# Last graph layer: the probabilities become the stationary operand of the weighing

## The chip, the cores and the metric

The kernel runs on one core of a Trainium2 chip. The metric is the device time of one execution in microseconds (us). Before the change it is 2272.47 us, the median of three runs (2269.34 to 2274.48).

## What is computed

The reference runs four graph layers over 1250 nodes with 512 features and 20,000 edges. The change touches only the last one, a graph attention with 8 heads of 64 features:

```python
for h in range(8):
    Wx = x @ Ws[h] + Wb[h]
    s = leaky_relu(Wx[v_tgt] @ a_w[h, :d] + Wx[v_src] @ a_w[h, d:] + a_b[h], 0.2)
    alpha = _segment_softmax(s, v_tgt, n)
    outs.append(segment_sum(alpha[:, None] * Wx[v_src], v_tgt, num_segments=n))
return stack(outs, axis=1).reshape(n, -1)
...
x = _layernorm(x + _L3_gnn_ref(...))
```

The kernel does this densely: for each head it makes a 1250 x 1250 matrix of exponentials, with the logarithm of the number of edges between two nodes added to the score, and multiplies it with the values Wx. A column of ones beside the values gives the sum of the exponentials, by which the result is divided.

## The kernel before, in words

The layer is `fourth_layer`. Nodes are cut into 10 tiles of 125 (TILE, TILES; HALF is 5). After a set-up (turning the nodes, the score rows, the values `values[source, tile, head, 65]` with their column of ones) come 80 steps: step T is head h = T // 10 and source tile j = T % 10. In a step the 125 sources of the tile lie on the partitions and all 1250 targets along them. All operands of the weighing are fp32, and each fp32 matmul appears in the trace as two passes, that is two weight loads and two matmuls.

One step passes these engines:

- POOL adds the logs of the counts and the targets' shifts (L2033, `logs_and_shifts`, two buffers).
- DVE combines that with the spread target scores in PSUM banks 3 to 5 (L2134, into `probabilities_turned`, four buffers). It waits for POOL, and for the weighing of four steps earlier (`pv`).
- ACT takes the exponential in place (L2208).
- PE weighs (L2307, `weigh`): the values of the tile (125 x 65) are stationary and the 1250 probabilities stream through in cuts of 512, 512 and 226, summed over the ten steps of the head in PSUM banks 0 to 2, 65 partitions by 1250 columns.

DVE has a second task between those: for the head after, it looks for each source tile's peak over the neighbours (L2071, `peaks`, 30 a head: 20 with 512 columns and 10 with 226), reading scores that PE spreads into bank 6 (L2258, `spread_sources`, three times a head). The peaks of a head run six steps ahead. In step j = 4 DVE works out the shifts (`shift_of`, L2079 to L2087), PE turns them (L2276, `shift_turned`) and spreads them in three pieces (L2282, `shift_piece`, steps 5, 6 and 7), all through bank 7, and ACT copies each piece (L2190). At j = 0 PE spreads the target scores of the new head (L2265, `spread_targets`) once DVE's last step of the old head is done.

The end of a head, before the change: ACT copies the 65 x 1250 sums out (L2198, `copy_out`, in step j = 0 of the next head), and the first weighing of the next head waits for that copy, since it writes the same banks. In steps 2 and 3 PE turns the copy back (L2297, `turn_back`, five transposes of 65 x 125 each time) into bank 7, in steps 3 and 4 DVE divides (`out_part`: L2099, L2101, L2106), and in steps 5 and 6 POOL adds the result to the nodes (L2025, `join`). `shift_turned` of the next head shares bank 7 with this and so waits for `parted` of both halves.

The order of the work on every engine is written out by hand. PE's order in a step is: target scores (j = 0), source scores (j = 4, 7, 0), shifts (j = 4) or a piece (j = 5, 6, 7), the weighing of the step before, a turning back (j = 2, 3). After the last step come the copy, the turning back, the division, the join, the row statistics, the norm and the output.

Of the kernel before, what the change touches and what calls it, by code (L numbers as in the profile page):

```python
# [9 lines left out]
ACT = mybir.ActivationFunctionType  # L10
AX = mybir.AxisListType
F32 = mybir.dt.float32
# [5 lines left out]
NODES, DIM, EDGES = 1250, 512, 20000  # L18
TILE = 125
TILES = NODES // TILE  # L20
# [10 lines left out]
CUTS = [(0, 512), (512, 1024), (1024, NODES)]  # L31
# [4 lines left out]
HEADS3, HDIM3 = 8, 64  # L36
# [6 lines left out]
def packer(nc, start):  # L43

    at = [start]

    def place(name, shape, dtype):
        size = int(np.prod(shape[1:])) * (2 if dtype in (BF16, F16) else 4)
        t = nc.alloc_sbuf_tensor_at(name, shape, dtype, offset=SBUF_BASE + at[0])
        at[0] += -(-size // 32) * 32  # L50
        return t

    return place
# [576 lines left out]
LAST_AT = WORK_AT + TILES * DIM * 4 + 640  # L630
# [1291 lines left out]
def fourth_layer(nc, fx, lw, psum, out):  # L1922
# [5 lines left out]
    with ExitStack() as ctx:  # L1928
        def sem(name):
            return ctx.enter_context(nc.semaphore("L3_" + name))  # L1930
# [26 lines left out]
        prob = packer(nc, TURNED_AT)("probabilities_turned", [128, 4, NODES], F32)  # L1957
        shifts = packer(nc, TURNED_AT + PLANE)("target_shifts_spread", [128, 2, NODES], F32)
        offset = packer(nc, SLOT_A_AT + TILES * NODES * 4 + 16)("logs_and_shifts", [128, 2, NODES], F32)
        weighted = packer(nc, LAST_AT)("weighted_values_turned", [128, 2, NODES], F32)  # L1960

        stored = sem("stored")
        turned, x_copied, picked, ones_set = sem("nodes_turned"), sem("turned_copied"), sem("selector_ready"), sem("ones_set")
# [6 lines left out]
        shift_own, shift_ready = sem("shift_step"), sem("shifts_ready")  # L1970
        piece, piece_copied = sem("spread_pieces"), sem("spread_pieces_copied")
        offset_ready, scored, exped, pv = sem("offsets_ready"), sem("scored"), sem("exped"), sem("weighted")
        out_copied, last_copied, back = sem("weighted_copied"), sem("last_weighted_copied"), sem("weighted_turned_back")
        part_own, parted, joined = sem("part_or_row_scale_step"), sem("parts_ready"), sem("nodes_joined")
        stat_own, var_ready, std_ready = sem("stats_step"), sem("variance_ready"), sem("std_ready")
        scale_ready = sem("row_scales_ready")
# [3 lines left out]
        def bank(n):  # L1980
            return psum[:, n * BANK:(n + 1) * BANK]

        def cols(t):
            return slice(t * TILE, (t + 1) * TILE)
# [4 lines left out]
        def region(n):  # L1989
            return psum[:, n * BANK:n * BANK + NODES]  # L1990

        def back_bank(h, k):

            return bank(6 if (h, k) == (HEADS3 - 1, 1) else 7)

        def reach_of(h):

# [3 lines left out]
        PEAKS = 3 * TILES  # L2001
# [39 lines left out]
        def _(dve):  # L2041
# [51 lines left out]

            def out_part(h, k):

                view = back_bank(h, k)[0:TILE, 0:HALF * WIDTH].rearrange("p (t d) -> p t d", d=WIDTH)
                m, v, n = mass[0:TILE, k, :], inverse[0:TILE, k, :], 2 * h + k
                dve.wait_ge(back, n + 1)
                dve.tensor_scalar(m, view[:, :, HDIM3:WIDTH].rearrange("p t d -> p (t d)"), 1e-30, None, ALU.max).then_inc(part_own, 1)  # L2099
                dve.wait_ge(part_own, 2 * n + 1)  # L2100
                dve.reciprocal(v, m).then_inc(part_own, 1)  # L2101
                dve.wait_ge(part_own, 2 * n + 2)
                if h >= 1:

                    dve.wait_ge(joined, n - 1)
                dve.tensor_tensor(part[0:TILE, k], view[:, :, 0:HDIM3], v.unsqueeze(2).broadcast_to([TILE, HALF, HDIM3]),  # L2106
                                  ALU.mult).then_inc(parted, 1)
# [19 lines left out]
            for T in range(STEPS):  # L2127
                h, j = T // TILES, T % TILES
                dve.wait_ge(offset_ready, T + 1)
                if j == 0:  # L2130
                    dve.wait_ge(target_spread, h + 1)
                if T >= 4:
                    dve.wait_ge(pv, T - 3)
                dve.scalar_tensor_tensor(prob[0:TILE, T % 4, :], region(3)[0:TILE], bend[0:TILE, j, h:h + 1],  # L2134
                                         offset[0:TILE, T % 2, :], ALU.max, ALU.add).then_inc(scored, 1)
                if j == TILES - 6 and h < HEADS3 - 1:
                    shift_of(h + 1)
                if h >= 1 and j in (3, 4):
                    out_part(h - 1, j - 3)
                g, at = (T + AHEAD) // TILES + 1, (T + AHEAD) % TILES  # L2140
                if g < HEADS3:
                    for n in range(PEAKS_AT[at], PEAKS_AT[at + 1]):
                        peaks(g, n)
                if h == HEADS3 - 1 and j in STATS_AT:
                    kept_stats(*STATS_AT[j])
            kept_stats(HALF, TILES)
            dve.wait_ge(pv, STEPS)
            a, z = CUTS[1]
            dve.tensor_copy(weighted[0:WIDTH, (HEADS3 - 1) % 2, a:z], region(0)[0:WIDTH, a:z]).then_inc(last_copied, 1)
            for k in range(2):  # L2150
                out_part(HEADS3 - 1, k)

# [21 lines left out]
        def _(act):  # L2174
# [14 lines left out]
                act.wait_ge(piece, 4 * h + 2 + k)  # L2189
                nc.scalar.activation(shifts[0:TILE, h % 2, a:z], bank(7)[0:TILE, 0:z - a], ACT.Copy).then_inc(piece_copied, 1)  # L2190

            def copy_out(h):

                act.wait_ge(pv, TILES * (h + 1))
                if h >= 2:
                    act.wait_ge(back, 2 * h - 2)
                for a, z in ((0, NODES),) if h < HEADS3 - 1 else CUTS[0::2]:
                    nc.scalar.activation(weighted[0:WIDTH, h % 2, a:z], region(0)[0:WIDTH, a:z], ACT.Copy).then_inc(out_copied, 1)  # L2198

            shift_turned(0)  # L2200
            for k in range(3):
                shift_piece(0, k)
# [2 lines left out]
            for T in range(STEPS):  # L2205
                h, j = T // TILES, T % TILES
                act.wait_ge(scored, T + 1)
                nc.scalar.activation(prob[0:TILE, T % 4, :], prob[0:TILE, T % 4, :], ACT.Exp,  # L2208
                                     bias=column[0:TILE, j, HEADS3 + h:HEADS3 + h + 1], scale=1.0 / UNIT3).then_inc(exped, 1)
                if j == 0 and h >= 1:  # L2210
                    copy_out(h - 1)
                if h < HEADS3 - 1:
                    if j == 4:
                        shift_turned(h + 1)
                    if j in (5, 6, 7):
                        shift_piece(h + 1, j - 5)
            copy_out(HEADS3 - 1)
            for k in range(2):
                at = half(k)
                act.wait_ge(var_ready, HALF * (k + 1))  # L2220
# [9 lines left out]
        def _(pe):  # L2230
# [37 lines left out]
            def shift_turned(h):  # L2268
                if h == 0:
                    pe.wait_ge(cols_ready, 2)  # L2270
                elif h == 1:
                    pe.wait_ge(piece_copied, 4)
                else:
                    pe.wait_ge(parted, 2 * h - 2)
                pe.wait_ge(shift_ready, h + 1)
                pe.transpose(bank(7)[0:TILES, 0:TILE], shift[0:TILE, h % 2, :], fx.ident[0:TILE, 0:TILE]).then_inc(piece, 1)  # L2276

# [5 lines left out]
                                   start=True, stop=True)  # L2283
                mm.then_inc(piece, 1)

            def turn_back(h, k):

                pe.wait_ge(out_copied, h + 1 if (h, k) != (HEADS3 - 1, 1) else HEADS3 + 1)
                if h == HEADS3 - 1:
                    pe.wait_ge(last_copied, 1)  # L2290
                    pe.wait_ge(peaked, PEAKS * HEADS3)
                if k == 0:
                    pe.wait_ge(piece_copied, 4 * min(h + 2, HEADS3))
                elif h < HEADS3 - 1:
                    pe.wait_ge(parted, 2 * h + 1)
                for t in range(HALF):
                    mm = pe.transpose(back_bank(h, k)[0:TILE, t * WIDTH:(t + 1) * WIDTH], weighted[0:WIDTH, h % 2, cols(k * HALF + t)],  # L2297
                                      fx.ident[0:WIDTH, 0:WIDTH])
                mm.then_inc(back, 1)

            def weigh(T):
                h, j = T // TILES, T % TILES
                pe.wait_ge(exped, T + 1)
                if j == 0 and h >= 1:
                    pe.wait_ge(out_copied, h)
                for a, z in CUTS:
                    mm = pe.matmul(region(0)[0:WIDTH, a:z], values[0:TILE, j, h, :], prob[0:TILE, T % 4, a:z],  # L2307
                                   start=(j == 0), stop=(j == TILES - 1))
                mm.then_inc(pv, 1)

            value(0)
# [19 lines left out]
            for T in range(STEPS):  # L2331
                h, j = T // TILES, T % TILES
                if j == 0 and h >= 1:
                    spread_targets(h)
                g, at = (T + AHEAD) // TILES + 1, (T + AHEAD) % TILES
                if g < HEADS3 and at in (0, 3, 6):
                    spread_sources(g, at // 3)
                if h < HEADS3 - 1:
                    if j == 4:
                        shift_turned(h + 1)  # L2340
                    if j in (5, 6, 7):
                        shift_piece(h + 1, j - 5)
                if T >= 1:
                    weigh(T - 1)
                if h >= 1 and j in (2, 3):
                    turn_back(h - 1, j - 2)
            weigh(STEPS - 1)
            for k in range(2):
                turn_back(HEADS3 - 1, k)


_INS = ("x", "src", "dst", "edge_weight", "node_vec1", "L0_gnn_W", "L1_gnn_f_w1", "L1_gnn_f_b1", "L1_gnn_f_w2",
# [47 lines left out]
```

## Time and profile before

| | |
|---|---|
| time, median of three runs | 2272.47 us |
| time of the profiled execution | 2274.44 us |
| its span | 2272.7 us |
| last layer's 80 steps, first DVE step to last weighing | 1992.09 to 2254.93 us |
| time from the start of one head's target scores to the next, heads 2 to 5 | 33.98 to 33.99 us each |
| mean granted TensorE clock | 0.968 |

The span is the profiler's, from the first to the last instruction; the time beside it is 1.74 us longer. "Busy" is the time in which an engine had an instruction running. PEclk is the share of the full TensorE clock that was granted: 1.00 is 2.4 GHz, 0.50 is 1.2 GHz. PEld is TensorE's weight load, which can run beside a matmul.

### The profile page before, as it was taken

Reading aid. Unit: us, or ns where it says so; the run is one execution under the profiler, and the core shown is the slowest. Engines: PE = TensorE matmul, PEld = TensorE weight load, DVE = VectorE, ACT = ScalarE, POOL = GpSimd, SP = SyncE. Lnnn points to the kernel's source line nnn. Section 1 sums busy time; section 2 is a strip of 40 time slices with the busy share of each in tenths; the row PEclk is TensorE's granted clock in tenths of the full one; section 3 lists DMA queues with packets and bytes.
Section 4 is the critical chain, followed back from the end, with each engine's and each line's share of the span. In section 5 each row is a group of like instructions: output and inputs, shape, how many; then the busy total and the mean of one; then the engine's idle time right before and its main releaser. Section 6 shows DMA issues by size and latency. Waiting matters only on the chain. (4 is left out here: it accounts for less than half of the span.)

```text
span 2272.7 us, 39837 instructions
## 1 busy us (share of the span) xinstructions
PE 2066.5 (91%) x15006; PEld 1608.6 (71%) x15006; DVE 1573.7 (69%) x3095; ACT 957.0 (42%) x1444; POOL 665.8 (29%) x488
## 2 busy tenths in 40 slices
PE   5999979899899999899999899999898996978886
PEld 4899937788788888788888787888785554433332
DVE  6789754778764778764777765678855235699985
ACT  0222213666333666433666433666420023045444
POOL 0000015300554200554210554200350000088785
PEclk9999989999999999999999999999999997999998
DMA  2000041789711698811688812588963300000001
GB/s 75 24 25 36 32 143 60 133 143 154 157 47 52 120 151 144 171 44 55 112 150 149 177 34 65 99 147 148 205 153 90 68 12 22 0 1 1 0 1 46
DMA packets 490381, 195.82 MB, mean 86 GB/s; under 512 B 441767, under 2 KB 460199, under 8 KB 490195
## 3 DMA queue, kind: packets, MB, share of 16 engines
q1 hardware_dynamic: 490195, 193.31, 41.8%
q8 instruction: 121, 1.98, 0.4%
q14 instruction: 65, 0.53, 0.1%
HBM read 62.94 MB, written 25.45 MB: 39 GB/s over the span
## 5 line engine op out<-in xcount | busy, mean ns | idle before, releaser
L720 PE MATMUL psum<-turned_probability_parts,values_high 125*128 125x125 bf16 x1600 | 278.6, 221 | 49.9 <-DMA turned_probability_parts<-probability_parts 23.2
L922 DVE CUSTOM_DVE_ANT_0 probabilities<-psum,counts 125x1250 f32<-125x1250 f32 x160 | 233.5, 1460 | 114.9 <-PE psum L722 114.6
L1480 ACT ACTIVATE probabilities<-probabilities,row_peaks 125x1250 f32<-125x1250 f32 x160 | 214.5, 1341 | 176.2 <-DVE row_peaks L926 176.2
L722 PE MATMUL psum<-turned_probability_parts,values_low 125*128 125x125 bf16 x1600 | 277.8, 220 | 0.0
L721 PE MATMUL psum<-turned_probability_parts,values_high 125*128 125x125 bf16 x1600 | 277.6, 220 | 0.0
L1680 DVE SCALAR_TENSOR_TENSOR probability_parts<-probabilities,row_masses,probability_parts 125x1250 bf16<-125x1250 f32 x160 | 251.6, 1573 | 13.5 <-ACT probability_parts L1492 13.3
L2033 POOL TENSOR_TENSOR logs_and_shifts<-logs_by_source,target_shifts_spread 125x1250 f32<-125x1250 f32 x80 | 208.2, 2619 | 107.3 <-ACT target_shifts_spread L2190 67.9
L1492 ACT ACTIVATE probability_parts<-probabilities,row_masses 125x1250 bf16<-125x1250 f32 x160 | 214.1, 1338 | 46.4 <-DVE row_masses L934 43.1
L2307 PE MATMUL psum<-probabilities_turned,values_and_ones 125*65 125x512 f32 (+1 forms) x480 | 190.1, 540 | 23.5 <-ACT probabilities_turned L2208 13.1
L720 PEld LDWEIGHTS psum<-turned_probability_parts,values_high 125*128 125x128 bf16 x1600 | 158.0, 99 | 73.8 <-issue 67.9
L2307 PEld LDWEIGHTS psum<-probabilities_turned,values_and_ones 125*65 125x65 f32 x480 | 63.6, 142 | 136.2 <-issue 113.7
L705 ACT ACTIVATE norm_std<-norm_moments,norm_eps 125x1 f32<-125x1 f32 x110 | 32.2, 294 | 299.9 <-DVE norm_moments L701 299.7
L721 PEld LDWEIGHTS psum<-turned_probability_parts,values_high 125*128 125x128 bf16 x1600 | 158.5, 99 | 0.0
L722 PEld LDWEIGHTS psum<-turned_probability_parts,values_low 125*128 125x128 bf16 x1600 | 158.4, 99 | 0.0
L2208 ACT ACTIVATE probabilities_turned<-probabilities_turned,score_columns 125x1250 f32<-125x1250 f32 x80 | 106.8, 1338 | 121.7 <-DVE probabilities_turned L2134 121.6
L457 PE MATMUL psum<-onehot_band,onehot_source 125*128 x2200 | 138.1, 226 | 16.6 <-DVE onehot_band L390 16.6
L457 PEld LDWEIGHTS psum<-onehot_band,onehot_source 125*128 125x128 bf16 x2200 | 131.2, 102 | 17.8 <-issue 17.1
L720 PE MATMUL psum<-turned_high,head_weights 128*128 128x512 f32 (+1 forms) x384 | 137.0, 357 | 3.7 <-POOL head_weights L1080 2.1
L722 PE MATMUL psum<-turned_high,head_weights 128*128 128x512 f32 (+1 forms) x384 | 136.1, 355 | 0.0
L721 PE MATMUL psum<-turned_low,head_weights 128*128 128x512 f32 (+1 forms) x384 | 136.1, 354 | 0.0
L2134 DVE SCALAR_TENSOR_TENSOR probabilities_turned<-psum,source_bends,logs_and_shifts 125x1250 f32<-125x1250 f32 x80 | 121.1, 1515 | 20.8 <-POOL logs_and_shifts L2033 12.9
L2071 DVE CUSTOM_DVE_ANT_0 masked_source_scores<-psum,absent_edges_by_target 125x512 f32<-125x512 f32 (+1 forms) x240 | 128.2, 584 | 9.3 <-PE psum L2258 9.3
(335 smaller groups left out, 5061.0 us busy)
## 6 DMA issues: line engine op xcount, KB each, us to landing
weight_stage<-in_L_gnn_m_w SPq DMA_DIRECT2D x32, 256.0 KB, 2.9
block_inputs_kept<-nodes SPq DMA_DIRECT2D x8, 896.0 KB
counts_kept<-counts_by_target_rows SPq DMA_DIRECT2D x10, 625.0 KB, 3.1
logs_kept<-counts SPq DMA_DIRECT2D x1, 5468.8 KB
nodes<-block_inputs_kept SPq DMA_DIRECT2D x12, 448.0 KB
turned_probability_parts<-probability_parts SPq DMA_TRANSPOSE x320, 3.6
counts_by_target<-counts_kept SPq DMA_DIRECT2D x2, 2187.5 KB
logs_by_source<-logs_kept SPq DMA_DIRECT2D x1, 4375.0 KB
```

What stands on the lines that cost most here:

```text
L457: mm = pe.matmul(region(b)[:, k * 128:(k + 1) * 128], onehot[0:TILE, q, k * TILE:k * TILE + 128], station[0:TILE, bass.ds(at, 1), q, :, :] ...
L720: pe.matmul(out, lh, rh, start=first, stop=False, skip_group_check=True)
L721: pe.matmul(out, lh, rl, start=False, stop=False, skip_group_check=True)
L722: return pe.matmul(out, ll, rh, start=False, stop=last, skip_group_check=True)
L922: dve.tensor_tensor_reduce(prob[0:TILE, T % 2, :], scores, fx.count_src[0:TILE, i, 0:NODES], scale, MASKED, ALU.add, ALU.max, p[:, 0:1]).t ...
L1480: nc.scalar.activation(prob[0:TILE, T % 2, :], prob[0:TILE, T % 2, :], ACT.Exp, bias=fx.peak[0:TILE, T % 2, 1:2], accum_out=fx.mass[0:TILE ...
L1492: nc.scalar.activation(parts[0:TILE, T % 2, 0:TILES, 0:TILE], by_tile(prob[0:TILE, T % 2, :]), ACT.Copy, scale=fx.mass[0:TILE, i, 2:3]).th ...
L1680: dve.scalar_tensor_tensor(parts[0:TILE, T % 2, TILES:2 * TILES, 0:TILE], by_tile(prob[0:TILE, T % 2, :]), fx.mass[0:TILE, i, 2:3], parts[ ...
L2033: nc.gpsimd.tensor_tensor(offset[0:TILE, T % 2, :], lw.logs[0:TILE, j, :], shifts[0:TILE, h % 2, :], ALU.add).then_inc(offset_ready, 1)
L2071: dve.tensor_tensor_reduce(masked[0:TILE, N % 2, 0:z - a], bank(6)[0:TILE, 0:z - a], lw.mask[0:TILE, t, a:z], 1.0, MASKED, ALU.add, ALU.ma ...
L2134: dve.scalar_tensor_tensor(prob[0:TILE, T % 4, :], region(3)[0:TILE], bend[0:TILE, j, h:h + 1], offset[0:TILE, T % 2, :], ALU.max, ALU.add ...
L2307: mm = pe.matmul(region(0)[0:WIDTH, a:z], values[0:TILE, j, h, :], prob[0:TILE, T % 4, a:z], start=(j == 0), stop=(j == TILES - 1))
```

## The change

The two operands of the weighing change places. In `weigh` a 125 x 125 block of the probabilities becomes stationary and the 65 columns of the values stream through it, ten times a step, so that the sums come out with the targets on the partitions: 125 x (5 x 65) for each half of the targets, in one bank. The halves n = 2h + k use banks 0, 1 and 2 in turn. `copy_out`, `turn_back`, the buffer `weighted_values_turned` and their semaphores go. `out_part` reads the sums where PE left them, waits for `pv` of the whole head, and moves from steps 3 and 4 to steps 1 and 2. A weighing that starts a bank for the fourth time or later waits for `parted` of the half that used it before. `shift_turned` no longer waits for `parted`, only for the copies of its own bank.

```diff
-        def back_bank(h, k):
-            return bank(6 if (h, k) == (HEADS3 - 1, 1) else 7)
+        def rows_bank(h, k):
+            return bank((2 * h + k) % 3)
...
             def out_part(h, k):
-                view = back_bank(h, k)[0:TILE, 0:HALF * WIDTH].rearrange("p (t d) -> p t d", d=WIDTH)
+                view = rows_bank(h, k)[0:TILE, 0:HALF * WIDTH].rearrange("p (t d) -> p t d", d=WIDTH)
...
-                dve.wait_ge(back, n + 1)
+                dve.wait_ge(pv, TILES * (h + 1))
...
-                if h >= 1 and j in (3, 4):
-                    out_part(h - 1, j - 3)
+                if h >= 1 and j in (1, 2):
+                    out_part(h - 1, j - 1)
...
-            dve.wait_ge(pv, STEPS)
-            a, z = CUTS[1]
-            dve.tensor_copy(weighted[0:WIDTH, (HEADS3 - 1) % 2, a:z], region(0)[0:WIDTH, a:z]).then_inc(last_copied, 1)
...
-            def copy_out(h):
-                act.wait_ge(pv, TILES * (h + 1))
-                if h >= 2:
-                    act.wait_ge(back, 2 * h - 2)
-                for a, z in ((0, NODES),) if h < HEADS3 - 1 else CUTS[0::2]:
-                    nc.scalar.activation(weighted[0:WIDTH, h % 2, a:z], region(0)[0:WIDTH, a:z], ACT.Copy).then_inc(out_copied, 1)
...
             def shift_turned(h):
                 if h == 0:
                     pe.wait_ge(cols_ready, 2)
-                elif h == 1:
-                    pe.wait_ge(piece_copied, 4)
                 else:
-                    pe.wait_ge(parted, 2 * h - 2)
+                    pe.wait_ge(piece_copied, 4 * h)
...
             def weigh(T):
                 h, j = T // TILES, T % TILES
                 pe.wait_ge(exped, T + 1)
-                if j == 0 and h >= 1:
-                    pe.wait_ge(out_copied, h)
-                for a, z in CUTS:
-                    mm = pe.matmul(region(0)[0:WIDTH, a:z], values[0:TILE, j, h, :], prob[0:TILE, T % 4, a:z],
-                                   start=(j == 0), stop=(j == TILES - 1))
+                for t in range(TILES):
+                    k, at = t // HALF, (t % HALF) * WIDTH
+                    if j == 0 and t % HALF == 0 and 2 * h + k >= 3:
+                        pe.wait_ge(parted, 2 * h + k - 2)
+                    mm = pe.matmul(rows_bank(h, k)[0:TILE, at:at + WIDTH], prob[0:TILE, T % 4, cols(t)], values[0:TILE, j, h, :],
+                                   start=(j == 0 and t % HALF == 0), stop=(j == TILES - 1), skip_group_check=True)
                 mm.then_inc(pv, 1)
...
-                if h >= 1 and j in (2, 3):
-                    turn_back(h - 1, j - 2)
             weigh(STEPS - 1)
-            for k in range(2):
-                turn_back(HEADS3 - 1, k)
```

## Rows read from the trace of the kernel before

**Rows 1.** The page: busy time of each engine over the span.
```profile
PE 2066.5 (91%) x15006; PEld 1608.6 (71%) x15006; DVE 1573.7 (69%) x3095; ACT 957.0 (42%) x1444; POOL 665.8 (29%) x488
```

**Rows 2.** By head: length, busy PE, PEld, DVE, ACT, POOL, then PEclk, DMA, GB/s.
```profile
1992.09:2023.00 30.91, 25.30 (x78) 10.26 (x78) 29.51 (x70) 15.14 (x15) 25.88 (x11) 0.89 0.00 0
2023.00:2056.05 33.05, 28.10 (x99) 12.45 (x98) 32.06 (x82) 15.89 (x16) 28.13 (x13) 1.00 0.00 1
...
2090.04:2124.03 33.99, 29.72 (x98) 12.83 (x98) 32.16 (x82) 16.23 (x16) 28.10 (x13) 0.95 0.00 0
...
2192.00:2224.85 32.85, 28.61 (x97) 12.51 (x96) 21.55 (x47) 16.68 (x16) 29.48 (x13) 0.95 0.00 1
2224.85:2254.93 30.08, 26.06 (x80) 10.07 (x79) 21.80 (x26) 14.37 (x11) 22.29 (x10) 1.00 0.00 1
```

**Rows 3.** Who waited for whom, 2090.04 to 2124.03: us, times, longest.
```profile
PE psum L2276 <- DVE output_part L2106: 1.8, 1, 1.8
PE psum L2307 <- ACT weighted_values_turned L2198: 1.4, 1, 1.4
...
DVE masked_source_scores L2071 <- PE psum L2258: 0.9, 1, 0.9
...
DVE output_masses L2099 <- PE psum L2297: 0.7, 1, 0.7
...
PE psum L2258 <- DVE neighbour_peaks L2071: 0.6, 1, 0.6
PE psum L2307 <- ACT probabilities_turned L2208: 0.4, 1, 0.4
```

**Rows 4.** The chain that ended last, in order of time: start, us, what.
```profile
1922.86 5.29 PE psum L2235 x24
...
1996.38 8.06 PE psum L2307 x18
...
2101.91 1.43 DVE probabilities_turned L2134
...
2105.41 3.79 PE psum L2307 x6
2109.21 1.08 PE psum L2282 x8
2110.29 2.24 PE psum L2307 x6
...
2117.03 0.60 DVE masked_source_scores L2071
...
2227.31 10.34 POOL logs_and_shifts L2033 x4
```

**Rows 5.** Groups of instructions by form, the layer's steps: busy us, mean ns, idle before.
```profile
L2033 POOL TENSOR_TENSOR logs_and_shifts<-logs_by_source,target_shifts_spread 125x1250 f32<-125x1250 f32 x80 | 208.2, 2619 | 107.3 <-ACT target_shifts_spread L2190 67.9 <-DVE probabilities_turned L2134 39.4
...
L2208 ACT ACTIVATE probabilities_turned<-probabilities_turned,score_columns 125x1250 f32<-125x1250 f32 x80 | 106.8, 1338 | 121.7 <-DVE probabilities_turned L2134 121.6
```

**Rows 6.** The timeline, TensorE's weight loads in three places: start, us, count.
```profile
279.07 2.31 PEld L493 LDWEIGHTS psum<-weights,nodes 125*128 125x128 f32 x20
...
2080.46 0.14 PEld L2307 LDWEIGHTS psum<-probabilities_turned,values_and_ones 125*65 125x65 f32 x1 [0.29 <-issue]
...
2255.69 1.17 PEld L2297 LDWEIGHTS psum<-identity,weighted_values_turned 65*125 65x125 f32 x10 [1.20 <-ACT weighted_values_turned L2198]
```

**Rows 7.** Three stretches with their granted clock, columns as in the second group.
```profile
279.00:289.00 10.00, 10.00 (x88) 9.67 (x86) 2.85 (x3) 2.74 (x7) 0.00 (x0) 1.00 0.38 144
1922.90:1927.80 4.90, 4.90 (x23) 4.18 (x24) 2.16 (x3) 2.66 (x5) 0.15 (x1) 0.50 0.01 2
...
2105.30:2108.70 3.40, 3.40 (x6) 0.93 (x5) 3.40 (x9) 0.27 (x1) 1.95 (x2) 0.51 0.00 0
```

**Rows 8.** The timeline at the end of the last head.
```profile
2252.58 2.32 PE L2307 MATMUL psum<-probabilities_turned,values_and_ones 125*65 125x512 f32 x6 [0.37 <-ACT probabilities_turned L2208]
...
2256.49 0.16 DVE L2099 TENSOR_SCALAR output_masses<-psum 125x5 f32<-125x5 f32 x1 [0.87 <-PE psum L2297]
```

More of the change, by code:

```diff
@@ L1959, in fourth_layer @@
         offset = packer(nc, SLOT_A_AT + TILES * NODES * 4 + 16)("logs_and_shifts", [128, 2, NODES], F32)
-        weighted = packer(nc, LAST_AT)("weighted_values_turned", [128, 2, NODES], F32)
         stored = sem("stored")
@@ L1972, in fourth_layer @@
         offset_ready, scored, exped, pv = sem("offsets_ready"), sem("scored"), sem("exped"), sem("weighted")
-        out_copied, last_copied, back = sem("weighted_copied"), sem("last_weighted_copied"), sem("weighted_turned_back")
         part_own, parted, joined = sem("part_or_row_scale_step"), sem("parts_ready"), sem("nodes_joined")
@@ L2209, in _ @@
                                      bias=column[0:TILE, j, HEADS3 + h:HEADS3 + h + 1], scale=1.0 / UNIT3).then_inc(exped, 1)
-                if j == 0 and h >= 1:
-                    copy_out(h - 1)
                 if h < HEADS3 - 1:
@@ L2216, in _ @@
                         shift_piece(h + 1, j - 5)
-            copy_out(HEADS3 - 1)
             for k in range(2):
@@ L2284, in shift_piece @@
                 mm.then_inc(piece, 1)
[L2286 to L2299, printed above, removed]
             def weigh(T):
@@ L2303, in weigh @@
                 pe.wait_ge(exped, T + 1)
-                if j == 0 and h >= 1:
-                    pe.wait_ge(out_copied, h)
-                for a, z in CUTS:
-                    mm = pe.matmul(region(0)[0:WIDTH, a:z], values[0:TILE, j, h, :], prob[0:TILE, T % 4, a:z],
-                                   start=(j == 0), stop=(j == TILES - 1))
+                for t in range(TILES):
[4 more added lines that the diff above has]
+                                   start=(j == 0 and t % HALF == 0), stop=(j == TILES - 1), skip_group_check=True)
                 mm.then_inc(pv, 1)
```

## The prediction

> **What bounds the kernel now.** I read the page first, then busy time head by head, the waits of one head, the chain that ended last, and last the timeline for the price of single passes. The page says that PE is busy 91% of the span [rows 1], but that is an average over four layers and says nothing of the last one. The cut by heads does [rows 2]: in a middle head of 33.99 us DVE is busy 32.16 us and PE 29.72. Four heads look like this one (2 to 5, 33.98 or 33.99 us). So in the middle heads DVE is nearly full, and what the change can give is what DVE waits, not what PE works.
>
> Those waits are two [rows 3]: 0.7 us for the transposes of the turning back, and 0.9 us for source scores (L2258) that PE delivered late. PE itself waits 1.4 us for ACT's copy at the start of the head, and 1.8 us at step 4 for the second `out_part`. The chain shows what follows that last wait [rows 4]: the next weighing takes 3.79 us instead of the 2.24 us of the one after, because the granted clock was at 0.51, its lower level (1.2 GHz), just then [rows 7]. PE is then behind by 1.55 us more, runs weighings and pieces back to back, and DVE waits 0.9 us at step 7. In head 1 the clock was 1.00 throughout and the head took 33.05 us [rows 2]: 0.94 us less, which is that second wait.
>
> Heads 6 and 7 have other limits. From step 4 of head 6 on there are no peaks (DVE busy 21.55 of 32.85 us), and PE's row of weighings and pieces is the limit. In head 7 the chain runs on POOL, four L2033 in 10.34 us.
>
> **The price of the new weighing.** A step had 3 matmuls of two passes, 6 passes; it will have 10 matmuls, 20 passes, each a load of 125 stationary columns and a stream of 65. The old step streams 2500 columns in passes: a 512-column pass starts every 0.14 + 0.29 = 0.43 us [rows 6], 0.84 ns a column, so 2.10 us, and 2.24 us with the load that shows at its start [rows 4]. For the new pass there are two rows of loads of that size. Twenty loads of 128 columns with 98 streamed take 2.31 us; less the last one's 0.19 over 19 steps that is 0.112 us a pass. These are plain fp32 matmuls on 125 rows, at clock 1.00. Ten loads of 125 columns with 65 streamed, the transposes of the turning back, take 1.17 us: (1.17 - 0.19) / 9 = 0.109 us [rows 6]. Streaming 65 columns is 0.055 us at 0.84 ns, hidden under the next load. I take 0.109: 20 x 0.109 = 2.18 us, plus 0.14 where the weighing starts after a break, 2.32 us at most against 2.24. The bounds are 0.109 and, if load and stream did not overlap at all, 0.109 + 0.055 = 0.164 us, 3.28 us a step.
>
> The Trainium skill ("TensorE: Matmul & The Clock Gate", Part 3, "What overlaps and what doesn't") says that a weight load overlaps a running matmul only when their row groups differ. Here they never differ, and by that rule the step would be the upper bound. The L493 rows have the same row groups on both sides and overlap all the same, so I go by the rows.
>
> PE's need in a middle head: 33.99 less its four waits (1.8 + 1.4 + 0.6 + 0.4 [rows 3]) is 29.8 us. Take off 1.55 for the slow stretch and 2 x 0.51 for the transposes, add 10 x 0.08 for the dearer steps: 28.0 us. DVE needs 33.99 - 0.7 - 0.9 = 32.4. PE keeps 4.4 us of slack, which is what hides the dearer steps; it is gone if a step costs over 2.32 + 0.44 = 2.76 us, 0.13 us a pass.
>
> **What goes, what moves.** I put DVE's step 0 of a head at 0. DVE needs 1.43 us a step and 0.60 for a large peak [rows 4], and some 0.31 for a small one (half the columns). With `out_part` (0.83 us) in steps 1 and 2, its steps start at 0, 2.4, 5.6, 8.5, 10.6, 15.3, 18.6, 21.8, 25.8, 29.1, and the next head at 32.3 to 32.4. POOL, at 2.62 us [rows 5], is ready before each of these.
>
> *The copy (ACT) and PE's wait of 1.4 us.* They go, but a wait takes their place: the bank of half k = 0 was freed in the last head, that of k = 1 is the one of `out_part(h-1, 0)`, on DVE at 3.9 to 4.7. PE starts this weighing at 2.9 (step of 1.5, exponential of 1.34 us [rows 5]), does five blocks by 4.1, stands 0.65 us and goes on to 5.9. Behind it on PE's queue are only weighings, whose exponentials come at 5.3 and 8.5. Worth: nothing, PE has slack there. For its part `out_part` waits for the last weighing of the old head, done at 2.8 (source scores of 0.4 from 0, then 2.3), a microsecond before DVE asks.
>
> *The turning back.* DVE's 0.7 us wait goes. Worth 0.7 a head.
>
> *`shift_turned` without `parted`.* PE waits for DVE's step 4 and the shifts (10.6 + 1.43 + 1.0 = 13.1), both `out_part` being done earlier; before it was 0.7 later, by the wait that went. PE itself has done the third weighing (exponential at 8.5, 2.3 us) and the source scores (0.4) at 11.2, so it stands 1.9 us, not less than the 1.8 of before: what came before the clock's drop stays. But the heads get 32.4 us long and each meets it in a new place; I take the drop in half of the heads. From 13.3 on PE has three weighings of 2.3 and two pieces of 1.08 [rows 4] before the source scores of step 7, and takes them up at 22.3; with the drop at 23.9, wanted at 23.3. So with the drop the wait stays, with 0.9 us at most, and without it it goes. DVE's step needs the weighing of four steps earlier, which is never late in either case.
>
> *The sum.* Head 0: nothing (no `out_part` and no turning back in it). Head 1, without a drop before: -0.7 for the turning back, 0.2 given back for a drop that may come now, -0.5. Heads 2 to 5: 0.7 plus half of 0.9, 4 x -1.15 = -4.6. Head 6: shifts turned 0.7 earlier, seven weighings of its PE-bound half 0.08 dearer (+0.6), half of the 1.55 us drop: -0.9. Head 7: POOL sets it; PE needs 2.3 of the 2.6 us. The end: the last weighing ends at 2254.90 and `out_part` starts at 2256.49 [rows 8]; it can start at about 2255.1, -1.4. Together -7.4 us. The profiled execution goes from 2274.44 (its span and 1.74 us around it) to 2267.0; the median of the runs shown is 1.97 lower, 2265.1. I say 2265. With all drops gone it is -0.7 - 6.4 - 1.7 - 1.4 = -10.2, with all of them there -2.8 - 0.1 - 1.4 = -4.3: its own range is 2261 to 2269.
>
> **The rivals.**
>
> *The clock stays low (slower).* Every weighing now streams only 0.055 of each 0.109 us; for the rest of it PE only loads. In the old weighing the streams fill the time. What the clock does over such a mix no row shows: it could stay at the lower level after the set-up (head 0 has a mean of 0.89 [rows 2]) or after the first drop. For it: nothing in the trace streams so little for long and is at 1.00. Against it: from 279 to 289 us PE loads 9.67 of 10 us, its streams of 98 columns fill 0.08 of each 0.11, and the clock is 1.00 [rows 7]. This lies between the old weighing and the new, so the case stays open. Price: at clock 0.50 a pass with 128 columns loaded took 5.29 / 24 = 0.220 us [rows 4, 7], so a pass costs 0.215 and a step 4.3 us. PE then bounds every head: 80 x 4.3 = 344 us, and what PE does beside it, 28.0 - 10 x 2.32 = 4.8 us at full clock and 9.6 at half, in each of seven heads, 67 us. That is 411 us from the first weighing at 1996.4 [rows 4], so the last ends at 2407 instead of 2255: 2272 + 152 - 1.4 = 2423, and 2400 to 2420 with some of it at the full clock. It decides as soon as the low level holds for three steps of a head: each costs PE 2.0 us, and it has 4.4.
>
> *Load and stream don't overlap (slower).* Step 3.28 us, PE 28.0 + 10 x 0.96 = 37.6 us a head, 7 x 37.6 + 33 = 296 us from 1996.4: 2293 instead of 2255, time 2309. Against it are both rows of loads; for it, only that neither has a stationary block of fresh data from ACT.
>
> *The gain is eaten.* The new wait on `parted`, the lag it gives PE, and a drop in every head, bring DVE new small waits, and only the end's 1.4 us and a little more are left: 2268 to 2273. For it: the head is tightly coupled, and PE's stand at step 4 is no shorter.
>
> **How the numbers follow.** 0.2% is 4.5 us here, about what a measurement of this kernel can tell from no change. Forecast 0.60; gain eaten 0.10; clock stays low 0.24; no overlap 0.06. So faster 0.60, same 0.10, slower 0.30. A range to 2309 would leave 0.24 out above, so it has to reach the clock's case: 2261 to 2420. The likeliest case's own range is 2261 to 2269.
>
> **What would show it.** A dense weighing should have 20 passes and start its loads 0.109 us apart. DVE's waits in a middle head should be under 1 us and the head 32.4 us, or 33.2 with a drop. PE should show two waits, 0.65 us at the second half of a head's first weighing and 1.9 us before L2276. L2099 at the end should come 0.2 us after the last weighing. The prediction is wrong if the granted clock in the steps is far below 0.9, or if passes are over 0.13 us apart.

## The result, and the profile after

The changed kernel takes 2410.2 us (median of 4 runs, 2409.95 to 2412.11) against 2272.71 us of the kernel before: a ratio of 1.0609, 95% interval 1.059 to 1.0627. It is 6% slower. The forecast of 2265 us was wrong, and the range up to 2420 holds the time only by way of the rival "the clock stays low".

The first two views are of the page of the changed kernel: busy time over the span, and the granted clock in 40 slices, in tenths.

```profile
PE 2235.4 (93%) x16046; PEld 1891.3 (79%) x16046; DVE 1574.3 (65%) x3094; ACT 948.8 (39%) x1435; POOL 663.1 (28%) x488
...
PEclk8999989999999999999999999999999795555555
```

DVE's busy time is what it was [rows 1]; PE's is 169 us more. The last seven slices, which are the last layer's steps and the end, are all at half clock. This is the busy time of heads 0, 1, 3, 6 and 7, as in [rows 2] (the columns are length, busy PE, PEld, DVE, ACT, POOL, then clock, DMA, GB/s):

```profile
1990.10:2039.13 49.03, 45.34 (x203) 43.22 (x203) 30.35 (x75) 16.27 (x15) 27.68 (x11) 0.50 0.00 0
2039.13:2090.24 51.11, 51.11 (x229) 48.58 (x228) 32.28 (x81) 15.08 (x14) 27.70 (x12) 0.50 0.00 1
2090.24:2141.34 51.10, 51.10 (x229) 48.58 (x228) 32.27 (x81) 15.09 (x14) 27.72 (x12) 0.50 0.00 1
2294.64:2344.20 49.56, 49.56 (x227) 48.03 (x226) 20.26 (x41) 14.64 (x14) 27.57 (x12) 0.50 0.00 1
2344.20:2392.00 47.80, 47.80 (x224) 47.09 (x223) 21.80 (x26) 14.66 (x11) 22.33 (x10) 0.50 0.00 1
```

A middle head takes 51.1 us instead of 33.99, and PE is busy in all of it, where DVE was the nearly full engine before. Head for head (the first counted from its first weighing, at 1996.38 us before and 1993.79 now) the layer lost 18.7 + 18.1 + 68.5 (heads 2 to 5) + 16.7 + 17.7 = 139.7 us. At the end 1.6 us came back, and what lies ahead of the first weighing was 2.6 us shorter in this execution. That leaves 135.5 us, the difference of the spans (2408.2 and 2272.7).

In the chain that ended last, a whole middle head (from the end of a weighing at 2090.10 us) is PE alone:

```profile
2090.31 1.34 PE psum L2249 x3
2091.64 0.21 PE psum L2242
2091.86 16.99 PE psum L2276 x80
2108.85 0.72 PE psum L2242
2109.57 0.30 PE psum L2258
2109.88 4.10 PE psum L2276 x20
2113.98 2.00 PE psum L2264 x8
2115.97 4.39 PE psum L2276 x20
2120.37 1.99 PE psum L2264 x8
```

L2276 is the weighing, L2264 a piece of the shifts (1.08 us in [rows 4], 2.00 now). Eighty passes in 16.99 us are 0.212 us a pass, twice the 0.109 that the load rows gave at full clock [rows 6]. The engines that waited in that head waited for PE:

```profile
DVE masked_source_scores L2069 <- PE psum L2242: 11.6, 2, 7.4
...
ACT target_shifts_turned L2180 <- PE psum L2258: 4.0, 1, 4.0
```

### The profile page after: what moved, and what is told of

The parts are those of the page before. It is cut to its first block and busy times, and to the rows that moved or that the text cites. A ratio compares the mean times of both kernels' runs of the same rounds, so it can differ in the third digit from the quotient of the medians.

```text
span 2408.2 us, 41883 instructions
## 1 busy us (share of the span) xinstructions
PE 2235.4 (93%) x16046; PEld 1891.3 (79%) x16046; DVE 1574.3 (65%) x3094; ACT 948.8 (39%) x1435; POOL 663.1 (28%) x488
## 5 line engine op out<-in xcount | busy, mean ns | idle before, releaser
L2276 PE MATMUL psum<-values_and_ones,probabilities_turned 125*125 125x65 f32 x1600 | 344.4, 417 | 7.1 <-ACT probabilities_turned L2195 7.1
L2276 PEld LDWEIGHTS psum<-values_and_ones,probabilities_turned 125*125 125x125 f32 x1600 | 338.7, 331 | 13.5 <-ACT probabilities_turned L2195 7.3
L705 ACT ACTIVATE norm_std<-norm_moments,norm_eps 125x1 f32<-125x1 f32 x110 | 32.2, 294 | 299.7 <-DVE norm_moments L701 299.6
```

The source lines that it names most:

```text
L2276: mm = pe.matmul(rows_bank(h, k)[0:TILE, at:at + WIDTH], prob[0:TILE, T % 4, cols(t)], values[0:TILE, j, h, :], start=(j == 0 and t % HALF ...
```

## Experiments

All compare with the kernel before on the same chip, which took 2273.8 us (median) beside e1 to e4, 2274.0 beside e5 to e8 and 2277.5 in its one run beside e9 and e10. The loads and the products that give the result are those of the changed kernel unless said otherwise.

**e1: twice the stream, the same loads.** Each pass but those of the very last weighing streams 130 columns of values instead of 65; the products of the second 65 go to unused columns of the same bank.

```diff
-                    mm = pe.matmul(rows_bank(h, k)[0:TILE, at:at + WIDTH], prob[0:TILE, T % 4, cols(t)], values[0:TILE, j, h, :],
+                    first, more = (j * HEADS3 + h) * WIDTH, WIDTH
...
+                        start_at, far = (2 * h + k) % 3 * BANK + at, 340 - at
+                        to = psum[0:TILE, start_at:start_at + 2 * far].rearrange("p (k c) -> p k c", k=2)[:, :, 0:WIDTH]
+                        moving = values[0:TILE].rearrange("p j h d -> p (j h d)")[:, first:first + 2 * WIDTH].rearrange("p (k c) -> p k c", k=2)
...
+                    mm = pe.matmul(to, prob[0:TILE, T % 4, cols(t)], moving,
```

> Changed kernel, but each pass streams 130 columns instead of 65 (the values of the next head too, their products go to unused columns of the same bank; only the very last tile of head 7 keeps 65). Loads, waits and order are the same. Theory (the clock stays low because the passes load more than they stream): clock in the steps back to about 0.95, passes 0.112 us apart, a middle head 32.4 to 33.3 us, time 2262 to 2271. Rival (something else in the new weighing holds the clock, such as the loads of 125 columns or the fp32 probabilities as stationary operand): clock 0.50 throughout and 2405 to 2420.

Measured: 2286.4 us, ratio 1.0055 (1.0038 to 1.0072). Nothing was taken from PE, its streams were doubled, and the time fell by 124 us. By stretch, head 1, which has no low stretch of the clock, and head 2, which has one:

```profile
2024.18:2056.42 32.24, 29.06 (x228) 26.31 (x227) 31.96 (x84) 14.87 (x15) 28.23 (x13) 1.00 0.01 2
2056.42:2097.61 41.19, 38.43 (x229) 35.05 (x228) 33.31 (x87) 15.89 (x15) 28.86 (x13) 0.75 0.00 1
```

So the loads of 125 columns and the fp32 probabilities as stationary operand don't hold the clock down; short streams with little else beside them do (e9 asks about the rest). The head at full clock takes 32.24 us. But 15 us above what was expected remain: two heads (2 and 3) take 41 us. The timeline of PE in head 2 shows the wait of step 4 (here L2258) and, in the 3.49 us of the weighing behind it, the clock's fall:

```profile
2068.50 0.50 PE L2242 MATMUL psum<-score_row_parts,row_selector 48*128 48x512 f32 x1
2070.66 0.27 PE L2258 MATMUL psum<-identity,target_shifts 125*10 125x125 f32 x1 [1.66 <-DVE target_shifts L2085]
2070.77 3.49 PE L2283 MATMUL psum<-values_and_ones,probabilities_turned 125*125 125x130 f32 x20
```

An earlier weighing (head 1), in the timeline of PE and of its loads, shows the passes at full clock, 30 loads in 3.40 us, (3.40 - 0.19) / 29 = 0.111 us each, and the wait on `parted` ahead of them:

```profile
2030.11 3.59 PE L2283 MATMUL psum<-values_and_ones,probabilities_turned 125*125 125x130 f32 x30 [0.44 <-DVE output_part L2104]
...
2030.11 3.40 PEld L2283 LDWEIGHTS psum<-values_and_ones,probabilities_turned 125*125 125x125 f32 x30 [0.64 <-DVE output_part L2104]
```

The wait of step 4 is about as long as before the change (1.66 us, 1.8 in [rows 3]), but the low level held for 20.5 us here and for 3.4 us in the kernel before. The wait alone does not decide it. Head 1 has the same wait, and this is its timeline:

```profile
2038.42 0.27 PE L2258 MATMUL psum<-identity,target_shifts 125*10 125x125 f32 x1 [1.67 <-DVE target_shifts L2085]
2038.53 2.38 PE L2283 MATMUL psum<-values_and_ones,probabilities_turned 125*125 125x130 f32 x20
```

PE stood 1.67 us, the weighing behind it took 2.38 us, and the clock stayed at 1.00. Of heads 1 to 6, each with a wait of 1.6 to 2.1 us, two had no drop (32.2 us), two had one of 3.4 us and two had one of 20.5 us.

**e2: a warm start.** Eight fp32 matmuls of 512 columns ahead of the first weighing, in a stretch in which PE otherwise stands for 7 us, into a bank that nobody reads.

```diff
+            for n in range(8):
+                pe.matmul(bank(2)[0:TILE], fx.ident[0:TILE, 0:TILE], lw.w_sb[0:TILE, n % CHUNKS, :], start=True, stop=True)
             for T in range(STEPS):
```

> Changed kernel with eight extra fp32 matmuls of 512 columns ahead of the first weighing, into a bank that nobody reads, in the stretch in which PE waits for the first probabilities. They should keep the clock at 1.00 to the first weighing. Theory (the mix itself cannot hold or regain the clock): the clock falls at one of PE's first waits, in head 0 or 1, and stays low, time 2390 to 2412. Rival (only the cold start is to blame, once warm the weighing keeps the clock): 2262 to 2275.

Measured: 2408.0 us in one run, as the theory expected. By stretch, from the first weighing on:

```profile
1993.30:1998.40 5.10, 3.60 (x31) 3.46 (x32) 5.08 (x17) 1.56 (x2) 3.41 (x3) 1.00 0.00 0
1998.40:2005.00 6.60, 6.60 (x32) 6.43 (x31) 4.72 (x15) 3.79 (x3) 6.60 (x3) 0.50 0.00 0
```

The weighings began at full clock, kept it for five microseconds in which PE stood for 1.5, and lost it before the long wait of step 4. It never came back. The cold start is not what keeps it low.

**e3: e1, and the weighing ahead of the wait.** In step 4 PE weighs first and then turns the shifts.

```diff
-                    if j == 4:
-                        shift_turned(h + 1)
...
                 if T >= 1:
                     weigh(T - 1)
+                if h < HEADS3 - 1 and j == 4:
+                    shift_turned(h + 1)
```

> As e1_wide, and in step 4 PE does the weighing before it turns the shifts, so that it doesn't stand with a ready weighing behind the wait. Theory: PE's stand of 1.9 us at step 4 goes, the clock does not drop there, DVE's wait for L2242 goes, a middle head takes 32.4 us, time 2260 to 2265, 2 to 6 us under e1_wide. Rival (no drops in e1_wide anyway, or the shifts come later and POOL or ACT wait for the pieces): same as e1_wide within 2 us.

Measured: 2268.81 us, ratio 0.9973 (0.9964 to 0.9983), the first version faster than both kernels. It is 17.6 us under e1, where 2 to 6 were expected, since e1's drops were so long. Behind the first weighings three drops are left, of 6.8, 10.2 and 3.4 us; PE now stands for ACT's copies ahead of the pieces (0.35 and 0.86 us in head 1). Heads without a drop take 32.23 us, the others 33.3 to 36.0.

**e4: the same change of order in the kernel before.** The diff is that of e3, with streams of 512 columns as they were.

> Kernel before with that one change of order alone. Theory (the clock's drop after PE's 1.8 us wait costs DVE 0.9 us in heads 2 to 5 and PE 1.5 us in head 6): 2266 to 2269, 4 to 6 us under before. Rival (the drop is not on the path): within 1.5 us of before.

Measured: 2272.17 us, ratio 0.9993 (0.9982 to 1.0003): no change that the runs can tell, where the theory expected 4 to 6 us. The wait only moved. This is PE's timeline in a middle head:

```profile
2070.03 2.32 PE L2307 MATMUL psum<-probabilities_turned,values_and_ones 125*65 125x512 f32 x6
...
2077.61 1.15 PE L2282 MATMUL psum<-target_shifts_turned,shift_row_selector 10*128 10x125 f32 x8 [1.40 <-ACT target_shifts_spread L2190]
```

PE stands 1.4 us for ACT's copy of the first piece instead, the clock still falls once in each of heads 2 to 5, for 3.4 us, and they take 34.1 us. Whether the drop alone is worth 0.9 us a head stays untested by this run, because it didn't remove the drop.

**e5 and e6: 98 columns, cold and warm.** The passes stream 98 columns, packed 98 apart in the bank; e6 has e2's extra matmuls too.

```diff
+                    wide = 98 if first + 98 <= TILES * HEADS3 * WIDTH else WIDTH
+                    at = (t % HALF) * 98
+                    mm = pe.matmul(rows_bank(h, k)[0:TILE, at:at + wide], prob[0:TILE, T % 4, cols(t)],
+                                   values[0:TILE].rearrange("p j h d -> p (j h d)")[:, first:first + wide],
```

> Changed kernel with 98 streamed columns a pass instead of 65 (33 columns of what lies behind the head's values, into the bank's free columns), the ratio of the L493 matmuls of the first layer, which ran at clock 1.00. Order and waits as in the changed kernel. Here the steps begin at the lower level. Theory (how much of the time the passes stream decides, and getting the clock back asks for more than keeping it): clock 0.50 to the end or nearly so, 2380 to 2412. Rival (any stream beyond half of the time is enough): 2265 to 2290.

> As e5, with the eight extra matmuls of 512 columns ahead of the first weighing, so that the steps begin at clock 1.00 as in e2. Theory: unlike e2 the clock stays at 1.00 through the first weighings; it falls at one of PE's longer waits (step 4 of head 0 or 1) and does not come back, 2370 to 2405. Rival (the start is all that e5 lacks): 2262 to 2280.

Measured: 2285.72 and 2299.55 us, one run each. Both expectations of the theory missed; e5 lies within the rival's range, and e6 within neither. By stretch of e5, the first weighings and what followed:

```profile
1990.00:1993.90 3.90, 3.90 (x20) 3.90 (x20) 3.69 (x9) 1.72 (x2) 3.90 (x2) 0.50 0.00 0
1994.10:2016.60 22.50, 21.57 (x180) 20.09 (x178) 20.38 (x47) 9.34 (x11) 16.18 (x8) 1.00 0.00 1
2016.67:2059.15 42.48, 39.44 (x229) 36.38 (x228) 33.37 (x87) 15.95 (x15) 30.12 (x13) 0.72 0.00 1
```

With 98 columns the clock does come back, even from the cold start, and falls again later as in e1 (three stretches of 20 to 24 us). In e6 the clock was kept from the start to 2038 us, but the warm start bought no time: e6 has five low stretches behind the start, 85 us together, where e5 has four with 68 us. The expectation had "getting the clock back asks for more than keeping it" and a clock of 0.50 nearly to the end; with 98 columns it came back within a few us of the first weighing.

**e7: e3, and the pieces behind the weighing too.**

```diff
+                    pass
+                if T >= 1:
+                    weigh(T - 1)
+                if h < HEADS3 - 1:
                     if j == 4:
                         shift_turned(h + 1)
                     if j in (5, 6, 7):
                         shift_piece(h + 1, j - 5)
-                if T >= 1:
-                    weigh(T - 1)
```

> As e3, and the three pieces of the shifts too come after the weighing of their step, so that PE does not stand for ACT's copies (0.4 and 0.9 us there in e3) with a ready weighing behind. Theory: fewer drops of the clock than in e3 (three), heads without one 32.2 us, time 2260 to 2266. Rival (the waits only move, drops as often): 2266 to 2272 as e3.

Measured: 2262.46 us, ratio 0.9949 (0.9933 to 0.9966). Three drops again, but of 3.4 us each, and the heads that have one take 32.9 us.

**e8: e7, with PE's waits filled.** One more matmul of 172 columns ahead of each weighing but a head's first.

```diff
+                if j >= 1:
+                    pe.matmul(bank(2 * h % 3)[0:TILE, 340:340 + 172], fx.ident[0:TILE, 0:TILE], lw.w_sb[0:TILE, 0, 0:172],
+                              start=False, stop=False, skip_group_check=True)
                 pe.wait_ge(exped, T + 1)
```

> As e7, with one extra fp32 matmul of 172 columns (two passes, 0.30 us) ahead of each weighing but a head's first, into columns that nobody reads. It costs PE 2.7 us a head, of the 4 to 5 us that PE stands. Theory: no drops in the steps, every middle head 32.2 us, 2259 to 2263. Rival (PE becomes the limit): heads of 33 us or more and 2266 or above.

Measured: 2261.02 us, ratio 0.9942 (0.9925 to 0.9958), the fastest here, though its interval and that of e7 overlap. From 1999 us to the last weighing the clock is 1.00 throughout:

```profile
2052.87:2085.10 32.23, 31.16 (x247) 28.78 (x246) 31.96 (x84) 15.09 (x15) 27.33 (x13) 1.00 0.01 1
...
1999.00:2242.90 243.90, 236.88 (x1886) 220.97 (x1886) 223.00 (x523) 114.72 (x105) 206.21 (x89) 1.00 0.01 1
```

**e9 and e10: 65 columns a pass, and three such extra matmuls.** This asks whether short passes themselves hold the clock, or how little PE streams altogether. The edit is e8's extra matmul on the changed kernel, in its order and with 65 columns, but three of them instead of one; e10 begins warm.

> Changed kernel, 65 columns a pass as in the changed one, and three extra fp32 matmuls of 172 columns (six passes, about 0.88 us at full clock) ahead of each weighing but a head's first, into columns that nobody reads. More work for PE, in matmuls of their own. Theory A (what counts is how much of a stretch PE streams, in whichever matmuls): the clock comes back at least for most of the time, PE then bounds a head at 37 us, time 2300 to 2340, under the changed kernel's 2410 though PE does more. Theory B (the short passes themselves hold the clock, whatever runs beside them): clock 0.50, a head of 66 us, time about 2530.

> As e9, with the eight extra matmuls ahead of the first weighing, so that the steps begin at clock 1.00. Theory A: the clock is kept in head 0 and most heads, 2295 to 2330. Theory B: it falls as in e2 and stays, about 2530. If e9 stays low and this one does not, keeping the clock asks for less than getting it back.

Measured: 2447.68 and 2454.33 us, one run each, between the two theories. By stretch of e9:

```profile
2034.04:2070.19 36.15, 35.23 (x283) 33.66 (x282) 32.14 (x81) 15.10 (x14) 28.07 (x13) 1.00 0.01 1
2299.13:2364.15 65.02, 65.02 (x280) 63.50 (x279) 20.34 (x41) 14.63 (x14) 27.62 (x12) 0.50 0.00 1
```

The loads of e9 in the first of these stretches, and e10 by stretch:

```profile
2035.74 3.39 PEld L2280 LDWEIGHTS psum<-values_and_ones,probabilities_turned 125*125 125x125 f32 x30
...
1979.50:2079.00 99.50, 96.30 (x706) 85.53 (x705) 84.14 (x216) 39.98 (x38) 74.38 (x32) 1.00 0.00 1
2079.20:2140.40 61.20, 61.20 (x260) 59.03 (x260) 30.62 (x79) 14.17 (x14) 26.53 (x12) 0.50 0.00 1
```

In e9 the clock came back after 24 us and held for 75 us, which takes in a whole head with the same 65-column passes, 36.15 us long; the second row is a later head at half clock, 65.02 us. It fell for 61 us, came back for 27 and then fell to the end. e10 kept it from its warm start to 2079 us, then lost it for 61 us, had it for 7 more and lost it to the end. So the short passes don't forbid the full clock; other streams beside them can bring it back and keep it for a time. At full clock the 65-column passes come (3.39 - 0.19) / 29 = 0.110 us apart, as e1's do with 130 columns: the longer stream costs nothing there, and the clock alone makes the 0.212 us of the changed kernel. As a remedy it failed: the extra work is paid in full, and the clock is kept only in part.

## Why the prediction was wrong, by its own steps

- **The step that failed** is the price of the weighing in the sum, "I take 0.109", which holds at full clock alone. The runs showed 0.212 us a pass at half clock, 4.27 us a step instead of 2.18, in all 80 steps. Behind it stands the choice between forecast and first rival: "This lies between the old weighing and the new, so the case stays open", with 0.24 for the clock staying low. The L493 stretch, with 98 columns streamed a pass, was taken as enough evidence against it. e5 shows that 98 columns get the full clock back, and e2 that 65, with nothing beside them, don't even keep it: the row was right about itself and said nothing of the change. That the new weighing streams for 0.055 us in a pass of 0.109 was worked out in the prediction itself.
- **The rival's mechanism and price** held. A pass was put at 0.215 us and measured 0.212 (80 passes in 16.99 us); PE's work beside the weighings was put at 9.6 us a head and measured 51.1 - 42.7 = 8.4 in a middle head. From the start of the first weighing to the end of the last the rival had 411 us, and it took 398.2 (1993.79 to 2392.01 us): 341 for the weighings instead of 344, and 57 for the rest instead of 67. That is the 13 us between 2423 and 2410. The 2.6 us by which the weighings began earlier about cancel against the rival's base, which was the median, 2.0 us under the profiled execution.
- **Load and stream overlap**: right. At full clock e1's passes, with 130 columns streamed, came 0.111 us apart, and at half clock in the changed kernel 0.212. The rule of the Trainium skill ("TensorE: Matmul & The Clock Gate", Part 3, "What overlaps and what doesn't") by which they would not overlap does not agree with this either: without overlap a pass of the changed kernel would take, by an estimate from the rows, about 0.109 + 0.055 us at full clock and twice that, 0.33, at half.
- **DVE as the bound, 32.4 us a middle head**: right where the clock is up. e1, e3, e7 and e8 show heads of 32.0 to 32.4 us there. DVE's 0.7 us wait for the turning back is gone in them.
- **The wait that takes the place of the copy's**: right. In e1 PE stands 0.44 us at the second half of a head's first weighing (0.65 was forecast), and it costs nothing.
- **PE's stand at step 4**: right in kind, 1.66 us in e1 for 1.9 forecast (in the changed kernel itself PE never stands there, being busy throughout). So was that only some of the heads would have a drop behind it: four of e1's heads 1 to 6 did. **What a drop costs** was wrong: 0.9 us a head, taken from the kernel before. With 130 columns a pass the low level held for 20.5 us and the head took 41.2 us, 9 us more. So even with the clock problem of the short streams out of the way the change would not have given 2265, but e1's 2286; only with the order of e3 or e7 besides does the time come to the forecast's size (2268.8 and 2262.5).
- **The end, -1.4 us**: -1.6. In the changed kernel `out_part` (L2097) starts at 2392.03 us, right after the last weighing, and the span ends 16.2 us after that weighing instead of 17.8.

That the clock is the cause, and that the short streams keep it low, is shown by e1 (same loads, waits and order, only the streams longer, -124 us), by e2 (not the start) and by e9 (the same passes at full clock 0.110 us apart). Why a low stretch lasts 3.4 us at one place and over 20 at another is not settled: behind the first weighings, stretches of 20 us and more came only in kernels with the new weighing, but e1, e3 and e7 have short ones too, and e1 has waits without any. In e8 none began between 1999 us and the last weighing.

## What to carry to other kernels

When stationary and moving operand change places, count for each pass how long it loads and how long it streams. If the stream is much the shorter one, ask first which granted clock the trace shows for such a mix, and if no row is as extreme, treat the half clock as a full case with its price worked out, not as a side risk. Longer streams, even of columns that nobody needs, can be free where the pass is bound by its load. And try the weighing that is ready ahead of the wait: behind a stand of under 2 us e1's heads lost between nothing and 9 us, and the new order took 17.6 us off e1, though it gave nothing that the runs can tell in the kernel before (e4).

## What the runs showed of the hardware

- The granted clock stayed at 0.50 from 1990 us to the end of the span, though PE was busy all of the time in the steps by the profile (51.10 of 51.10 us in a middle head). A busy PE is no sign of a fast one.
- Passes of a 125-column fp32 load came 0.212 us apart at half clock with 65 columns streamed and 0.111 us at full clock with 130: doubling the streamed columns halved the time of a pass, by way of the clock. With 65 columns at full clock (e9) it was 0.110 us.
- From a start at 1.00 the clock fell after 5 us of weighings with 65 columns (e2). With 98 columns it rose from 0.50 within the first weighings (e5). In the kernel before it was at 0.50 too when the steps began, from 1992.80 to 1999.40 us, and at 1.00 behind that.
- The same stand of PE at step 4 had different consequences. In the kernel before, 1.8 us were followed by 3.4 us at half clock in heads 2 to 5 and by none in head 1. In e1, 1.63 to 1.67 us were followed by 20.5 us in heads 2 and 3, by 3.4 us in head 4 and by none in heads 1 and 5.
